# The last group of a decoder layer's second shared expert: its units before the former group's output products, and its sums and norms batch by batch

## The reference

```python
logits = x @ w_router.T; two of 8 experts per token, weights from sigmoid scores
out  = sum over the two chosen experts e:  weight * ((silu(x @ wg[e].T) * (x @ wu[e].T)) @ wd[e].T)
out += sum over the two shared experts j:  (silu(x @ sg[j].T) * (x @ su[j].T)) @ sd[j].T
y = layernorm(x + out)          # over the 256 features of a token, no weights
```

## Time and profile before

| | us |
|---|---|
| median of 3 runs | 755.33 (755.0 to 757.05) |
| span of the profiled execution, first to last instruction | 762.8 |
| the profiled execution's own time | not on the page |
| TensorE busy (share) | 705.9 (93%) |
| VectorE busy | 565.6 (74%) |
| ScalarE busy | 475.1 (62%) |
| GpSimd busy | 345.7 (45%) |

### The profile page before, as it was taken

How to read it: one execution, slowest core, us unless ns; L and a number is a source line. 1 busy time by engine, 2 the same in 40 slices (tenths; PEclk the granted TensorE clock), 3 DMA queues, 4 the chain that set the end, 5 groups by cost and what they waited for, 6 DMA issues and landing times.

```text
span 762.8 us, 15120 instructions
## 1 busy us (share of the span) xinstructions
PE 705.9 (93%) x4958; PEld 640.0 (84%) x4958; DVE 565.6 (74%) x1176; ACT 475.1 (62%) x1068; POOL 345.7 (45%) x512
## 2 busy tenths in 40 slices
PE   4998888897999999999999999999899999999965
PEld 3888676686889999999999988879899999999855
DVE  4873788886878787878787878683877877876436
ACT  4544755456777777777777777451777777775301
POOL 0001666687998787878787883071000000000431
PEclk9999999999999999999999999999999999999978
DMA  9001500010200000000240030085476667660221
GB/s 300 2 1 50 207 1 1 1 34 28 63 9 1 8 0 7 0 7 0 69 144 0 0 104 2 4 289 174 144 237 220 205 232 240 195 210 28 63 62 56
DMA packets 45939, 64.81 MB, mean 85 GB/s; under 512 B 4288, under 2 KB 34880, under 8 KB 45632
## 3 DMA queue, kind: packets, MB, share of 16 engines
q1 hardware_dynamic: 40080, 56.45, 22.3%
q0 software_dynamic: 1536, 4.20, 1.7%
q10 hardware_dynamic: 4272, 3.51, 1.6%
HBM read 53.14 MB, written 11.01 MB: 84 GB/s over the span
## 4 chain that ended last, share of the span: by engine, by line
PE 61%; POOL 7%; DVE 5%; issue 4%; ACT 2%; POOLq 0%; DVEq 0%; ACTq 0%
PE two L67 9%; PE two L69 7%; PE two L68 7%; PE bg L67 7%; PE bg L69 7%; PE bg L68 7%; PE bd L67 4%; PE bd L69 4%; PE bd L68 3%; PE two L321 3%; POOL under_dt L595 1%; PE two L296 1%; POOL under_raw L581 1%; POOL under_raw L576 1%; POOL wo_lo L599 1%
## 5 line engine op out<-in xcount | busy, mean ns | idle before, releaser
L1921 POOL DMA_INDIRECT gu_raw<-rows_out,slot x16 | 15.7, 984 | 199.9 <-issue 199.9
L414 ACT ACTIVATE under_dt<-two,nb,under_raw 128x256 f32<-128x256 f32 x128 | 70.6, 561 | 43.0 <-DVE nb L497 43.0
L2032 ACT ACTIVATE sg<-bg 128x256 f32<-128x256 f32 (+1 forms) x95 | 40.8, 429 | 89.3 <-PE bg L69 83.2
L67 PE MATMUL bg<-xb_hi,gu_hi 128*128 128x256 f32 x300 | 86.1, 287 | 2.9 <-DVE xb_lo L2149 2.9
L69 PE MATMUL bg<-xb_hi,gu_lo 128*128 128x256 f32 x300 | 84.8, 283 | 0.0
L68 PE MATMUL bg<-xb_lo,gu_hi 128*128 128x256 f32 x300 | 84.8, 283 | 0.0
L2126 DVE TENSOR_TENSOR hf<-sg,bg 128x256 f32<-128x256 f32 (+1 forms) x95 | 45.0, 473 | 47.5 <-ACT sg L2032 44.2
L67 PE MATMUL two<-under_h 128*128 128x256 f32 (+1 forms) x208 | 66.5, 320 | 2.9 <-PEq L118 1.5
L67 PE MATMUL bd<-dn_hi,eh_hi 128*128 128x256 f32 x220 | 62.7, 285 | 3.4 <-issue 3.4
L595 POOL TENSOR_SCALAR under_dt<-under_dt,rec 128x256 f32<-128x256 f32 x128 | 62.8, 510 | 6.4 <-DVE rec L543 6.4
L69 PE MATMUL bd<-dn_hi,eh_lo 128*128 128x256 f32 x220 | 62.5, 284 | 1.8 <-issue 1.8
(11 more groups left out here) (296 smaller groups left out, 2533.2 us busy)
## 6 DMA issues: line engine op xcount, KB each, us to landing
gu_raw<-in_gu SPq DMA_DIRECT2D x17, 1280.0 KB
dn_raw<-in_dn SPq DMA_DIRECT2D x17, 640.0 KB
rows_in<-under_dt SPq DMA_DIRECT2D x1, 3840.0 KB, 13.1
rows_out<-y_sb SPq DMA_DIRECT2D x30, 128.0 KB, 2.1
x_blk<-rows_in ACTq DMA_DIRECT2D x13, 256.0 KB, 2.7
under_raw<-in_wq SPq DMA_DIRECT2D x1, 2048.0 KB, 7.6
under_raw<-in_wkv SPq DMA_DIRECT2D x1, 2048.0 KB, 12.2
under_raw<-in_wo SPq DMA_DIRECT2D x4, 512.0 KB, 3.9
```

Of the source, the lines that this page charges most:

```text
L67: pe.matmul(out, lh, rh, start=first, stop=False)
L414: act.activation(self.prob[:, g % 2, h, :], self.b_s[:, h // 2, (h % 2) * MW:(h % 2 + 1) * MW], ACT.Exp, bias=self.nb[:, h:h + 1], scale=s ...
L2032: act.activation(sg[:, u % 3, 0:width(u)], gate_of(u), ACT.Silu).then_inc(f_sg, 1)
```

## The change

Three parts. On TensorE, in group 18 all five units run before `down(17)`, and `down(18)` follows it. `down(18)` goes tile by tile, each tile into its own `bg` bank, after one wait for all units. On VectorE the four `add_last` and `norm_stats` of batches 0 to 3 and `norm(0)` leave their places between the units; after the last `rest_h`, each batch gets `add_last` and `norm_stats` in turn, with `norm(0)` after batch 4, `norm(1)` after 6, `norm(2)` and `norm(3)` after 7. The last root group is split in two, batch 6 and batch 7. The mixes stay where they are: mix(2) to mix(5) ahead of gated(92), mix(6) and mix(7) ahead of gated(94).

```diff
-    ROOTS = ((0, 4), (4, 6), (6, 8))
+    ROOTS = ((0, 4), (4, 6), (6, 7), (7, 8))
...
         def last_out(t):
-            return (bd[0], bd[1], bx[0], bx[1])[t][:, 0:DM]
+            return bg[t][:, 0:DM]
...
                 if q == NG_ - 1:
-                    for i in range(IT):
-                        pe.wait_ge(f_hlo, IT * q + i + 1)
-                        for t in range(4):
-                            if i == 0 and t < 2:
-                                pe.wait_ge(f_acc, BATCH + 2 * t + 2)
-                            elif i == 0:
-                                pe.wait_ge(f_xlo, NBLK)
-                            ts = slice(t * P, (t + 1) * P)
+                    pe.wait_ge(f_h, IT * NG_)
+                    pe.wait_ge(f_hlo, IT * NG_)
+                    for t in range(4):
+                        ts = slice(t * P, (t + 1) * P)
+                        for i in range(IT):
                             mm = products(pe, last_out(t), (h_hi[:, q % 2, i, ts], h_lo[:, q % 2, i, ts]),
                                           (dn_hi[c][:, i, :], dn_lo[c][:, i, :]), i == 0, i == IT - 1)
-                            if i == IT - 1:
-                                mm.then_inc(f_d, 1)
+                        mm.then_inc(f_d, 1)
                     return
...
-                if q >= 3:
+                if 3 <= q < NG_ - 1:
                     down(q - 1)
...
+            down(NG_ - 2)
             down(NG_ - 1)
...
                 if last:
                     for b in range(2, 6):
                         mix(b)
-                    for b in range(4):
-                        add_last(b)
                 if q > 1:
                     gated(IT * q + 2)
                 if 2 <= q <= NBLK:
                     rest_x(q - 1)
-                if last:
-                    for b in range(4):
-                        norm_stats(b)
                 if q:
                     gated(IT * q + 3)
                 rest_h(IT * q + 2)
                 if last:
                     mix(6)
                     mix(7)
-                    norm(0)
...
             rest_h(IT * NG_ - 1)
-            for n in (1, 2):
-                for b in range(*ROOTS[n]):
-                    add_last(b)
-                for b in range(*ROOTS[n]):
-                    norm_stats(b)
-            for n in (1, 2):
-                norm(n)
+            for b in range(BATCH):
+                add_last(b)
+                norm_stats(b)
+                if b >= 4 and b != 5:
+                    norm(max(b - 5, 0))
+            norm(len(ROOTS) - 1)
```

## The result

| | us |
|---|---|
| before, median (4 runs beside after) | 755.16 |
| after, median of 4 runs (761.68 to 762.18) | 762.16 |
| ratio after to before, with its 95% interval | 1.0083 [1.0069, 1.0096] |
| forecast | 760.2 |

The account below looks back on a forecast made before the run. TensorE, busy 93% of the span, was taken to bound the kernel. Its end 6.8 us later (wait for gathers, lower clock), less 1.9 us of tail, gave +4.9 on 755.33: 760.2 us, range 752.5 to 762.

Parts of the forecast that it names:

- Which before: Kernel's end rebuilt without the profile's single, paused matmuls (727.36 to 735.82): TensorE ends at 745.8, span near 754.2 us.
- rival A: Single matmuls are real in every execution and vanish with the change: faster by 3.7 us, to 751.6; chance 0.20.
- Step 1: Units 2 and 3 of group 18 move up on TensorE to 720.81, ending at 726.3, at no cost.
- Step 2: Unit 4 waits for gated(92), behind mix(5) on VectorE: TensorE idles 6.9 us, from 726.3 to 733.2.
- Step 3: TensorE's dense work after the long idle runs at a lower clock: 1.6 to 2.7 us lost, 2.15 taken.
- Step 4: Rest of TensorE, 17.1 us all dense, ends at 752.6; remaining unit work on VectorE and ScalarE is hidden.
- step 5: Group 18's products tile by tile: no new wait; VectorE's sums and first three normalised groups with stores hidden under products.
- the sign that the prediction named for step 5 being wrong: In the profile after, VectorE still at norm(0) or norm(1) when the last tile is ready.
- step 6: Tail from the last matmul to the span's end: 6.5 us instead of 8.4, so 1.9 gained.
- The sum: TensorE's end 6.8 us later, tail 1.9 us shorter: +4.9 us, giving 760.2 us.

Follow-up runs that it names:

- experiment 1: The kernel before, unchanged, profiled once more: 755.11 us, span 753.4.
- experiment 4: After, with TensorE's old order alone put back (products of group 17 between units 1 and 2 of group 18): 757.12 us, 1.0026 against before.
- experiment 8: experiment 6 with TensorE's old order (group 17's products between units 1 and 2) and VectorE's order fitted to it: 757.79 us, 1.0019 against before.
- experiment 2: After, with mix(2) to mix(7) moved behind the last rest_h on VectorE: 755.92 us, 1.0008 against before.
- experiment 5: After, with gated(92) alone moved ahead of mix(2) on VectorE: 757.92 us, 1.0027 against before.
- the spare matmuls: After, with 28 matmuls of overwritten result between units 3 and 4 of group 18, filling TensorE's wait: 759.33 us, 1.0045 against before.
- experiment 6: After, with VectorE's mixes spread among the last units' work and the batch sums, norm(0) after batch 5, other norms after batch 7: 751.95 us, 0.9958 against before.

## Why the prediction was right, and where its numbers were off
**Which before.** Right. The rebuilt end of TensorE, 745.8, was 745.09, and the rebuilt span, 754.2, was 753.4 (experiment 1). Most of that difference is that experiment 1 reached the end of unit 1 0.48 us earlier (720.33 against 720.81): from there to TensorE's end it took 24.8 us, 25.0 rebuilt. Beside rival A the prediction set a rule of the Trainium skill (Runtime: NRT & Kernel Launch, section The ~15µs preamble/postamble breakdown): a profile's total lies a nearly fixed 6 us above the reported time. No run here shows such a total. The spans here begin and end with the kernel's own instructions, and in the profiled runs of experiment 1 and of after the time lies 1.7 us above the span. What made the single matmuls in the first execution stays open: in experiments 1, 4 and 8 dense products ran beside the same gathers and none appeared.

**Steps 1 and 2.** Right. No cost for units 2 and 3; a gap of 6.95 us (6.9 forecast) behind gated(92), which followed mix(5). Experiments 2 and 5 take the wait away by another order alone and the gap goes.

**Step 3.** Right, 2.3 us by unit 4's rows against 2.15, 2.1 to 2.8 by the spare matmuls. The clock fell before unit 4 and rose at its end. The Trainium skill says the same (TensorE: Matmul & The Clock Gate, section HAM oscillation — how this bites in real kernels): a long pause of TensorE throttles it, and what follows starts at half rate; the trace agrees, 0.51 over 733 to 738.

**Step 4.** Right: TensorE's end 752.80 against 752.6. The end is 7.7 us later than in experiment 1, where 6.8 were forecast. 0.34 us of that lies ahead of the change (unit 1 ended at 720.67 and at 720.33); counted from there TensorE ends 7.4 us later, 0.6 more than forecast.

**Steps 5 and 6, mis-sized.** "batch 6 with norm(1) 1.7, done within about 0.1 us of the end of the last tile": norm(1), started at 752.87, stood ahead of add_last(7), which began at 753.52, while the last matmul had ended at 752.80. That is the sign that the prediction named for step 5 being wrong; and norm(2) ran behind the last matmul too, so of three normalised groups only the first was hidden. The tail was 7.2 us instead of 6.5, against 8.3 in before: 1.1 us gained, not 1.9. VectorE was late for two reasons. Step 5 had it free 5.4 us before the end of the products, at 747.4, but it came to add_last(4) at 747.73, because the sums of batches 2 and 3 waited for the late products of group 17 (to 745.60). And norm(0) waited 0.55 us for GpSimd's root (row at 749.36), which could only start when batch 3 was summed; step 5 put that wait at nothing. In experiment 6, where VectorE is not late, the tail is 6.6 us, against 6.5 forecast.

**The sum.** 7.7 - 1.1 = 6.6 us in spans (753.4 to 760.0), 7.0 in medians, 4.9 forecast: 0.9 from the two ends of TensorE (0.3 of it ahead of the change), 0.8 from the tail, the rest between spans and medians. Sign and mechanism were right; of the size, the tail's gain in steps 5 and 6 was the term most in error.

## What to carry to other kernels
Before moving work on one engine, ask what waits it was filling: here 7.2 us of products that needed nothing hid a wait for gathers, and moving them behind the units laid it bare. In a fixed order an instruction that waits for a DMA holds back all that stands behind it; put it behind the instructions that free another engine's buffers, and only then reorder that other engine. Sums that are moved behind the last unit make their own engine the next limit (experiments 2, 4 and 5). And set a profiled span against the timed runs before adding to it.

## What was not expected of the hardware
A wait of TensorE of 3.26 us (experiment 4) and one of 3.28 (experiment 5) were followed by full clock, one of 3.43 (experiment 8) by the lower level, 0.50 from 740 to 744, which cost 2.4 us: of three nearly equal waits one brought the clock down. A shorter wait went both ways too: behind the 2.65 us of the earlier trace rows the clock was at the lower level, and all other profiles show this again, but in experiment 1 the same wait, 2.64 us before 175.47, had 1.00 behind it (175.5 to 178.4). And one execution of an unchanged kernel showed matmuls one by one for 8.5 us (727.36 to 735.82), with no wait in the trace to explain it, which no other profile repeated.
